# Layer 0's keys are scaled by sine and cosine on Pool instead of VectorE

## The reference

```
q = relu(x Wq + bq);  k = relu(x Wk + bk);  v = x Wv + bv
idx = pi/2 * [1..L] / L
k_ = concat(k * sin(idx), k * cos(idx))      # per token
q_ = concat(q * sin(idx), q * cos(idx))
kv = sum over tokens of k_ v^T;  z = 1 / max(q_ . sum(k_), eps)
out = (q_ kv) * z, then Wo
```

## Time and profile before

| what | value |
|---|---|
| median of 3 runs | 1235.9 us (1235.37 to 1239.16) |
| profiled execution, its own time | 1238.85 us |
| profiled execution, span from first to last instruction | 1237.4 us |
| mean granted clock of PE | 0.972 of full speed |
| busy: PE, DVE, ACT, POOL | 1159.9, 901.3, 925.2, 636.0 us |
| of it on DVE: L1079, 128 instructions | 37.2 us |

### The profile page before, as it was taken

The page is one execution under the profiler, slowest core; times in us unless marked ns, Lnnn a source line. Parts: engine busy times, 40 slices in busy tenths (PEclk is TensorE's granted clock), DMA queues, the critical chain, the costliest instruction groups (busy, mean ns, idle before and its releaser), DMA issues.

```text
span 1237.4 us, 28621 instructions
## 1 busy us (share of the span) xinstructions
PE 1159.9 (94%) x9792; PEld 690.6 (56%) x9792; DVE 901.3 (73%) x2439; ACT 925.2 (75%) x1352; POOL 636.0 (51%) x857
## 2 busy tenths in 40 slices
PE   6768999999999999999999999999997889899998
PEld 4344454545454545455454545454543476799998
DVE  4548888888888888888888888888878463345554
ACT  2134888878788888888888888787875867667775
POOL 2442647464656555564646474646552202048886
PEclk9888999999999999999999999999997898999999
DMA  3760616233242616060605152442555300025543
GB/s 128 187 133 11 127 30 148 59 87 89 56 111 35 124 29 133 12 133 12 135 15 130 42 103 63 82 100 46 119 171 95 103 21 11 16 44 64 60 59 31
DMA packets 92947, 97.56 MB, mean 79 GB/s; under 512 B 12808, under 2 KB 72712, under 8 KB 92424
## 3 DMA queue, kind: packets, MB, share of 16 engines
q1 hardware_dynamic: 80104, 86.16, 31.1%
q0 software_dynamic: 12272, 8.92, 5.7%
q10 hardware_dynamic: 432, 0.66, 0.2%
HBM read 68.88 MB, written 26.23 MB: 77 GB/s over the span
## 4 chain that ended last, share of the span: by engine, by line
PE 68%; ACT 14%; DVE 9%; issue 6%; POOL 2%; DMA 0%; ACTq 0%; DVEq 0%; POOLq 0%
PE PS L843 10%; PE PS L688 10%; PE PS L803 9%; PE PS L638 6%; PE PS L770 5%; PE PS L854 5%; PE PS L788 5%; ACT flow L957 4%; ACT L957 3%; PE PS L619 3%; ACT qp L948 2%; PE PS L652 2%; PE PS L630 2%; PE PS L755 2%; ACT early L881 2%
## 5 line engine op out<-in xcount | busy, mean ns | idle before, releaser
L1397 POOL TENSOR_SCALAR_AFFINE_SELECT flow<-flow 128x256 f32<-128x256 f32 (+1 forms) x448 | 190.8, 439 | 352.1 <-ACT flow L957 348.6
L957 ACT ACTIVATE flow<-PS 128x1024 f32<-128x1024 f32 x320 | 319.8, 1028 | 30.5 <-PE PS L788 28.5
L1226 DVE TENSOR_REDUCE nm<-PS 128x2 f32<-128x1024 f32 x128 | 154.8, 1221 | 60.8 <-PE PS L755 60.7
L948 ACT COPY qp<-PS 2x512 f16<-2x512 f16 x256 | 147.4, 576 | 66.2 <-PE PS L778 63.6
L803 PE MATMUL PS<-flow 128*32 128x512 f32 (+3 forms) x2048 | 169.0, 449 | 2.1 <-POOL flow L1397 0.5
L1382 POOL TENSOR_TENSOR early<-early 128x512 f32<-128x512 f32 x120 | 152.4, 1293 | 6.6 <-DMA early<-gate_rows 6.2
L688 PE MATMUL PS<-early,down 128*128 128x512 f32 x288 | 147.9, 626 | 8.3 <-POOL early L1382 8.3
L638 PE MATMUL PS<-xnT,up 128*128 128x512 f32 x288 | 145.2, 607 | 0.0
L843 PE MATMUL PS<-xsT,w1s 128*128 128x128 f32 x1136 | 142.5, 280 | 0.4 <-DVE act L1324 0.3
L1421 POOL DMA_INDIRECT out_y<-X,rowu x71 | 110.5, 1556 | 60.1 <-DMA out_y<-X 33.7
L1228 DVE TENSOR_REDUCE nm<-PS 128x2 f32<-128x768 f32 x128 | 121.6, 950 | 25.8 <-PE PS L755 25.7
(11 more groups left out here) (164 smaller groups left out, 2002.1 us busy)
## 6 DMA issues: line engine op xcount, KB each, us to landing
early<-gate_rows SPq DMA_DIRECT2D x128, 256.0 KB, 5.1
qp<-relay_q SPq DMA_DIRECT2D x64, 128.0 KB
kp<-relay_k SPq DMA_DIRECT2D x64, 128.0 KB
xsb<-xs SPq DMA_DIRECT2D x71, 65.0 KB, 1.8
relay_k<-qkh SPq DMA_DIRECT2D x32, 128.0 KB, 6.3
out_y<-X SPq DMA_DIRECT2D x16, 256.0 KB, 5.9
early<-in_w SPq DMA_DIRECT2D x1, 4096.0 KB, 12.3
relay_q<-qkh SPq DMA_DIRECT2D x16, 128.0 KB, 2.3
```

The costliest lines, as they stand in the source:

```text
L948: ins = act.copy(m.qp[b % 2][at:at + 2, 2 * g + x, :], ps[turned:turned + 2, :])
L957: act.activation(m.pt[:, n % RING, :], m.PS[:, i:i + 2, :].rearrange("p k c -> p (k c)"), ACT.Exp, scale=1.0 / SCALE).then_inc(s["exp"], 1)
L1226: dve.tensor_reduce(nm[:, 3, 2 * n:2 * n + 2], ps, AX_X, ALU.max, negate=True).then_inc(s["max"], 1)
L1397: ins = pool.affine_select(part, part, [[0, part.shape[1]], [1, P]], ALU.is_ge, nothing, base=0, channel_multiplier=-1)
```

## The change

The two scalings of each tile leave DVE's part of the stage kvr. Pool gets a part of that stage, at the same place of the order: it waits for the bias instruction's semaphore, makes both scalings with the same operations and operands, and counts `ks`. DVE no longer waits for its own bias instruction.

```
@@ vector_program @@
         dve.tensor_tensor(m.kvr[:, t, :], wk(("kvr", b, t))[:, 0:KVW], m.bkv[:, :], ALU.add).then_inc(s["kvr"], 1)
-        dve.wait_ge(s["kvr"], b * NT + t + 1)
-        for sc in range(2):
-            ins = dve.tensor_scalar(m.ks[:, t, sc, :], m.kvr[:, t, 0:D], 0.0,
-                                    const(m, K_SC)[:, sc * NT + t:sc * NT + t + 1], ALU.max, ALU.mult)
-        ins.then_inc(s["ks"], 1)
@@ pool_program @@
+    def kvr(b, t):
+        pool.wait_ge(s["kvr"], b * NT + t + 1)
+        for sc in range(2):
+            ins = pool.tensor_scalar(m.ks[:, t, sc, :], m.kvr[:, t, 0:D], 0.0,
+                                     const(m, K_SC)[:, sc * NT + t:sc * NT + t + 1], ALU.max, ALU.mult)
+        ins.then_inc(s["ks"], 1)
+
-    share = dict(stats0=stats0, stats1=stats1, q=q, gated=gates, score=scores, rope=rope, sort=sort, scatter=scatter)
+    share = dict(stats0=stats0, stats1=stats1, kvr=kvr, q=q, gated=gates, score=scores, rope=rope, sort=sort, scatter=scatter)
```

## The result

| | before | after |
|---|---|---|
| median of 5 runs each, us | 1235.9 (1235.29 to 1239.16) | 1248.68 (1245.49 to 1253.29) |
| ratio to before, 95% interval | | 1.0097 (1.0081 to 1.0113) |
| profiled execution, span, us | 1237.4 | 1251.9 |
| period of the steady part, us | 58.24 | 59.25 |

The change makes the kernel 1.0% slower. The forecast was 1232.6 us, and the time lies outside its range.

What follows compares the result with a forecast made beforehand. PE, busy for 94%, was taken as the bound. Terms of -2.7 (12 steady batches), -0.48, +0.15 and -0.3 (first batches) sum to -3.3 us, off the 1235.9 median: 1232.6 us, range 1228.5 to 1241.

Steps and rivals of the forecast that it cites:

- What bounds the kernel: Steady batches: PE bounds, and only the first scaling pair delays it, through DVE's reduction, 2.7 us over 12 batches.
- Removed from DVE: DVE's kvr stage: first pair's removal gains PE 0.2 us a batch, 2.7 in all; the other three pairs nothing.
- Added to Pool: Price of one 128x128 scaling on Pool: 0.34 us, borrowed from the affine select; range 0.34 to 1.04.
- k: Time of one scaling on Pool, forecast as 0.34 us; the sign was to turn at 0.62.
- Pool's queue: Pool's order around the kvr stages: selects pushed back, but users come later and the rope is not delayed; no cost.
- The rival of the slow scaling: Pool's scaling slow, norm1 late for PE: 1241.4 us at 0.8 us a scaling, 1249 at 1.04; chance 15%.
- What the two engines do to each other: Norm1 beside Pool's first pair: ends at 567.01, PE gets it at 567.19 before needing it at 567.39; costs nothing.
- The first three batches: Start and windows at 51 and 103 us, unsaturated chains: -0.48, +0.15 and -0.3 us.

Runs made afterwards that it cites:

- tile0_on_dve: Changed kernel with tile 0's two scalings back on DVE, tiles 1, 2 and 3 still on Pool: 1249.28 us, 1.011.
- dve_tile0_later: Kernel before, nothing on Pool, with DVE scaling tile 0 together with tile 1, behind norm1: 1234.8 us, 0.9983.
- only_tile0_on_pool: Kernel before with only tile 0's two scalings on Pool, DVE keeping tiles 1, 2 and 3: 1233.36 us, 0.9974.
- immediate_factor: Changed kernel with the constant 0.5 as the factor of Pool's scalings instead of the token's sine or cosine: 1241.86 us, 1.0037.
- one_operation: Changed kernel with Pool's scaling as one product with the token's sine or cosine, without the maximum with zero: 1238.53 us, one run.
- one_op_constant: Changed kernel with Pool's scaling as one product with the constant 0.5, without the maximum with zero: 1233.48 us, one run.
- Tile3_on_dve: Changed kernel with tile 3's two scalings back on DVE, tiles 0, 1 and 2 still on Pool: 1236.38 us, 0.9998.
- rope_before_tile3: Changed kernel, all scalings on Pool, with tile 3's pair behind rope 0's addition in Pool's order: 1236.36 us, 0.9992.
- pool_gaps: Changed kernel, all scalings on Pool, with the pairs of tiles 2 and 3 behind rope 0's addition in Pool's order: 1238.61 us, 1.0017.
- two_halves: Changed kernel with each scaling on Pool split into two instructions of 64 columns: 1285.69 us, one run.
- qkh_behind_exponentials: Changed kernel with ACT's cast qkh, DVE's qkl and their transfers moved later in the order, behind score 18: 1251.26 us, 1.0112.

## Why the prediction was wrong, point by point

**What bounds the kernel, and "Removed from DVE": right.** The wait for the reduction was worth 0.2 us a batch. It is gone in the changed kernel, came back with the pair (tile0_on_dve), and gave 0.26 and 0.28 us of period where nothing replaced it (dve_tile0_later, only_tile0_on_pool). The other three pairs were worth nothing on DVE, as costed.

**"Added to Pool": the first step that failed.** k was taken as 0.34 us and is 0.71. The per-element rate was borrowed from the affine select, 0.89 ns, because both have one tensor input. Measured with the edits: 3.4 ns an element and 0.28 us at the start for this instruction; 713 ns as it stands, 71 less with a constant factor, 101 less with one operation (173 less with both, so the two add up). The start was near the 227 ns of the 4-element row; the rate was four times off. The Trainium skill (GPSIMD Engine Reference, "4.1 Engine selection") calls one-input elementwise work there "roughly line-rate". These runs don't bear it out for this instruction: 713 ns on Pool against 287 on DVE.

**"Pool's queue": the second, and the one that decided the sign.** The step laid the pairs out with k = 0.34 alone, found the fourth done before the rope's addition was due, and costed the queue at nothing. It kept 0.34 to 1.04 for the range, but didn't lay the queue out again at any other k. The rows would nearly have allowed it. Pool is released at 567.64; up to the rope it has two selects, three, and one (0.76 + 1.31 + 0.36 in the chain above) and six scalings of k. The addition starts at 567.64 + 2.43 + 6k = 570.07 + 6k. Before, it started at 573.21, with 0.07 us to spare, so PE is late from a start at 573.28 on, which is k = 0.54. Here k is the distance between scalings that follow each other, which is 0.03 to 0.05 us less than their length (575.05 to 577.80 for four: 0.69). With 0.69 the addition starts at 574.21 and L704 is 0.93 us late; the trace has 574.25, by the chain, and 0.94. Measured in the same way, against the residual sum, immediate_factor (k = 0.60) should be 0.39 late and is 0.43, one_operation (0.58) 0.27 and is 0.29, and one_op_constant (0.49) not late, and L704 comes 0.22 us earlier than before. Tile3_on_dve and rope_before_tile3 take pairs out of this stretch and the loss goes; tile0_on_dve takes out one that lies ahead of 567.64, and it stays.

That the selects pushed back by the second pair reach their user in time failed with it: in the same unbroken stretch the selects come late, and PE waits 0.2 us a batch for one of them at L803.

**The rival of the slow scaling: right side, wrong mechanism.** It named the right cause, k, with 15%. But it priced it by norm1 = 566.1 + 2k. At k = 0.71 that gives 567.52, and with its own 0.06 us up to PE 0.19 a batch, 2.3 us in twelve, where 12.8 came. (By that 0.06 us PE meets norm1 from k = 0.52 on, not from 0.49.) Its 1249 us for k = 1.04 is near the measured time by accident: k is smaller, and norm1 was not late.

**"What the two engines do to each other": in the steady part the term was not there.** It was to let norm1 end behind Pool's pair and two selects. It ended 0.2 us before Pool's pair was done. Over all of 200 to 880 us L1046 takes 353 ns on average against 350 before. In other places of these runs instructions do grow where the two engines run together: the first tile of norm1 took 3.03 us, the four of norm1 at 103 us took 1.38 us beside Pool's pair where they took 1.10 before, L1241 took 1.32 us in pool_gaps, and one of Pool's scalings took 1.22 us there. The Trainium skill (SBUF — State Buffer, "Who interferes with whom") lets whichever instruction comes first hold the shared ports for its whole length, and the other block. By that rule, for a VectorE instruction in a two-port mode, norm1's first would have waited for Pool's scaling of 571.95; it started at 572.07 and all four ended before Pool's second did. Which of Pool's instructions hold DVE up, and which don't, was not isolated.

**"The first three batches": half right.** The rows:

```profile
13.98 4.20 POOL L1354 TENSOR_SCALAR early<-early,kc 128x128 f32<-128x128 f32 x6 [0.38 <-DVE early L1076]
```

```profile
16.25 0.26 ACT L893 ACTIVATE e<-e 128x64 f32<-128x64 f32 x1 [6.13 <-DVE e L1090]
```

```profile
18.23 2.05 PE L652 MATMUL PS<-early 128*128 128x129 f32 x16 [0.71 <-POOL early L1354]
```

```profile
104.57 0.73 PE L619 MATMUL PS<-kc,xn 128*128 128x128 f32 x4 [2.90 <-DVE xn L1046]
```

The exponential came 0.49 us earlier, as forecast (-0.48). But Pool's last six scalings took 4.20 us in a row, kv waited 0.71 us for them, and the branch called the shorter became the longer: of 0.48 only 0.17 reached the next matmuls. At 51 us norm1 came 0.1 us later (+0.15 forecast), at 103 us PE took it up 0.1 us earlier in the batch (-0.3 forecast), since norm1 took 1.38 us, where the forecast's 102.81 to 104.0 leaves 1.19.

**The clock** was in no step. It is 3.1 us of the profiled execution's 14.5. The two falls came behind the new waits in this trace and none shows where those waits are absent (tile3_on_dve, rope_before_tile3). Of the kernels that have such waits, tile0_on_dve had one fall behind twelve of 0.80 us (a period of 60.88 us instead of 59.31) and two_halves three, but immediate_factor had twelve waits of 0.5 us and no fall, and qkh_behind_exponentials eleven of 0.86 us and none. No experiment set it alone, so what decides whether a wait is followed by a fall stays open.

## What to carry to other kernels

When work goes to another engine, lay out that engine's queue at both ends of the price's range, from the last instruction that something releases to the next one that somebody waits for, and write down from which price on it is late. Six scalings stood in that queue, so an error of 0.35 us for each became 2 us of queue and 1 us a batch. Take a duration from a row of the same instruction with the same number of elements, or take none, and don't borrow the rate of another with the same number of inputs. And move only the piece that the list of waits names: one pair of four gave 0.26%, all four cost 1.0%.

## What the runs showed of the hardware

- Pool's tensor_scalar of 128x128 f32: 713 ns with two operations and a factor per partition, 642 with a constant, 612 with one operation, 540 with both simplifications; 64 columns take 496. The number of operations and the kind of operand count on this engine, and a split in two costs 39% more (2 x 496 against 713).
- Pool's pair of 1.47 us beside DVE's four L1046 of 1.12 us left these at their length, while Pool's addition of 1.27 us held a DVE tensor_scalar of 0.17 us for 1.32 us, and a scaling of Pool's took 1.22 us instead of 0.71 beside a DVE tensor_tensor of 0.71 us (pool_gaps).
- A wait of 0.78 us before PE's matmuls was followed, in 2 of 12 batches, by a stretch at a granted clock of 0.50, 3.4 us in the one shown, worth 1.56 us each; eleven waits of 0.86 us in another order of ACT's work were followed by none.
